# Two attention and mixture-of-experts layers on one core: the last four source tiles of the second attention go to target chunk 0 first, and two routed tiles are run among the products of the others

## What is computed

```
z = s1[:, None, :] + s2[None, :, :]              # 2048 x 2048 x 4 heads
e = where(z > 0, z, 0.2 * z).mean(-1)
attn = softmax(where(adj > 0, e, -9e15), axis=1)
x = x + attn @ Wh

h = relu(layernorm(x) @ Wi.T + bi)               # 256 wide, routed block
for l in range(2):                               # one expert per 32 rows
    h = relu(shared_l(h) + routed_l(h) + h)
x = x + h @ Wo.T + bo
```

## Time and profile before

| what | value |
|---|---|
| time, median of 3 runs | 642.82 us (642.39 to 643.41) |
| the profiled execution | 641.88 us, its span 640.1 us |
| busy, share of the span | PE 85%, PEld 67%, DVE 81%, ACT 58%, POOL 27% |
| chain that ended last, by engine | PE 52%, DVE 26%, ACT 14%, issue 5% |
| its largest line | DVE L1633, 15% |

### The profile page before, as it was taken

The page is one execution under the profiler, slowest core; times in us unless marked ns, Lnnn a source line. Parts: engine busy times, 40 slices in busy tenths (PEclk is TensorE's granted clock), DMA queues, the critical chain, the costliest instruction groups (busy, mean ns, idle before and its releaser), DMA issues.

```text
span 640.1 us, 13281 instructions
## 1 busy us (share of the span) xinstructions
PE 545.5 (85%) x5082; PEld 427.7 (67%) x5082; DVE 515.6 (81%) x907; ACT 372.2 (58%) x756; POOL 175.9 (27%) x186
## 2 busy tenths in 40 slices
PE   1876984999999999799998897999996756999985
PEld 1675972878775877766685575588786555566753
DVE  6799969997787857699949738899999898999420
ACT  1796893768885777685756836633421301565473
POOL 3301000075211100993522010121314000365741
PEclk9987995989998899998998999899999878899999
DMA  6484860022165156999599224020102844475750
GB/s 142 85 161 76 215 153 2 17 83 68 33 199 198 38 195 215 186 211 237 119 209 110 67 69 131 2 67 1 66 1 80 303 134 139 120 208 175 202 165 16
DMA packets 48857, 78.36 MB, mean 122 GB/s; under 512 B 5406, under 2 KB 24870, under 8 KB 48794
## 3 DMA queue, kind: packets, MB, share of 16 engines
q1 hardware_dynamic: 30714, 52.02, 26.0%
q0 software_dynamic: 15488, 22.02, 20.1%
q10 hardware_dynamic: 2592, 3.48, 2.0%
HBM read 80.61 MB, written 22.06 MB: 160 GB/s over the span
## 4 chain that ended last, share of the span: by engine, by line
PE 52%; DVE 26%; ACT 14%; issue 5%; DMA 1%; ACTq 1%; POOL 0%; SPq 0%; DVEq 0%
DVE arena L1633 15%; PE bank L698 11%; PE bank L710 11%; PE bank L627 10%; PE bank L863 5%; ACT arena L1137 5%; PE bank L824 2%; ACT maskT L1006 2%; PE bank L658 2%; PE bank L900 2%; ACT ysb L1089 1%; PE bank L808 1%; PE bank L576 1%; PE bank L603 1%; DVE arena L1489 1%
## 5 line engine op out<-in xcount | busy, mean ns | idle before, releaser
L483 POOL TENSOR_TENSOR x<-x,ysb 128x512 f32<-128x512 f32 x36 | 74.7, 2076 | 249.8 <-ACT ysb L1089 237.7
L1137 ACT ACTIVATE arena<-heads,nd 128x512 bf16<-128x512 f32 x176 | 112.0, 723 | 22.9 <-PE bank L627 22.3
L698 PE MATMUL bank<-hTc,arena 128*128 128x512 f32 x192 | 92.9, 638 | 5.6 <-ACT reg_c L1078 5.6
L1633 DVE SCALAR_TENSOR_TENSOR arena<-reg_b,nd,arena 128x1536 f32<-128x1536 f32 x48 | 92.0, 1979 | 0.0
L710 PEld LDWEIGHTS bank<-arena,reg_c 128*128 128x128 f32 x768 | 87.6, 192 | 4.8 <-issue 4.7
L710 PE MATMUL bank<-arena,reg_c 128*128 128x128 f32 x768 | 88.5, 275 | 0.0
L627 PEld LDWEIGHTS bank<-reg_b,arena 128*128 128x128 bf16 x1536 | 73.7, 99 | 7.1 <-DVE arena L1489 4.0
L1078 ACT ACTIVATE reg_c<-bank,b 128x512 f32<-128x512 f32 x96 | 65.0, 686 | 22.8 <-PE bank L698 22.6
L627 PE MATMUL bank<-reg_b,arena 128*128 128x99 bf16 x1536 | 74.9, 211 | 3.7 <-DVE arena L1489 3.7
L1089 ACT ACTIVATE ysb<-bank,comb 128x128 f32<-128x128 f32 x128 | 36.5, 367 | 65.0 <-PE bank L909 39.9
L1475 DVE TENSOR_TENSOR arena<-maskT,arena 128x2048 bf16<-128x2048 bf16 x36 | 50.4, 1401 | 27.4 <-ACT arena L1137 27.4
(11 more groups left out here) (195 smaller groups left out, 846.6 us busy)
## 6 DMA issues: line engine op xcount, KB each, us to landing
maskT<-routed_sums SPq DMA_DIRECT2D x48, 256.0 KB, 3.2
reg_c<-in_adj POOLq DMA_DIRECT2D x16, 512.0 KB, 7.9
arena<-in_w1T SPq DMA_DIRECT2D x16, 512.0 KB, 4.0
arena<-in_w2T SPq DMA_DIRECT2D x16, 512.0 KB, 4.9
routed_sums<-in_wsT SPq DMA_DIRECT2D x32, 256.0 KB, 5.6
routed_sums<-in_wrT POOLq DMA_DIRECT2D x32, 256.0 KB, 13.9
arena<-routed_sums SPq DMA_DIRECT2D x32, 256.0 KB, 3.0
routed_sums<-ident POOLq DMA_DIRECT2D x4, 1024.0 KB, 12.6
```

The lines of the kernel that those rows point to most:

```text
L483: nc.gpsimd.tensor_tensor(xi, xi, ysb[:, e % 3, :].rearrange("p (t d) -> p t d", d=P), ALU.add).then_inc(s_acc, 1)
L698: mm(bank[b][:, :], w1[:, s, e % 2, c * P:(c + 1) * P], hTc[:, :], start=True, stop=True).then_inc(full[b], 1)
L1137: last = af(ind[:, q, b, j, :], sbc[:, h, :], ACT.Relu, bias=nd[:, q * QT + j, h:h + 1], scale=BIG)
L1633: last = v.scalar_tensor_tensor(p, row, nd[:, t, h:h + 1], p if h else maskT[:, t, columns], ALU.max, ALU.mult)
```

## The change

The pass over source tiles 12 to 15 is split by targets. First come 512 columns (chunk 0) of all four tiles and all heads, then 1024 columns (chunks 1 and 2), head by head; chunk 0 is merged and normalised on DVE between the first and the second head of these. PE takes the four tiles to chunk 0's bank space, then chunk 0's first pair of routed tiles in banks of its own (4 to 7), then the four tiles to the other targets. The `attend1` tiles are spread otherwise over the pairs. The loads of `kept` 0 to 11 go ahead of the small weights; the second-layer weights of tiles 0 and 1 get places of their own. The diff, cut to its core:

```diff
         def w_second(t, g):
             m = t % 2 * GT + g
+            if t < 2:
+                return (arena[:, 8848:9360], arena[:, 9360:9872], hT[:, WW:N], ysb[:, 2, :],
+                        *(rows1[:, h, 0:CW] for h in range(H)))[m].rearrange("p (k n) -> p k n", k=KC)
...
+        def tile_banks(t):
+            return ((4, 5), (6, 7))[t] if t < 2 else (2 + t % 2 * 2, 3 + t % 2 * 2)
...
+            sp.wait_ge(s_skip, 16 * L * KC)
+            for e in range(T - CT):
+                load_kept(e)
             sp.wait_ge(s_acc, FFN_Y)
...
+            sp.wait_ge(ev["rows"], 3 * H)
+            load_second(0)
+            sp.wait_ge(s_c0, CT)
+            load_second(1)
+            for e in range(T - CT, E1):
+                load_kept(e)
             load_second(2)
             load_second(3)
             sp.wait_ge(full[3], BANK3)
-            load_second(0)
-            load_second(1)
...
+            def attend_part(targets, t, ready):
+                pe.wait_ge(s_v1, C)
+                pe.wait_ge(ready, t + 1 if ready is s_wide else t - (T - CT) + 1)
+                for i in targets:
+                    b, o = i // 3, i % 3 * (P + 1)
+                    last = mm(bank[b][:, o:o + P + 1], wide[:, t % 4, i * P:(i + 1) * P], v1[:, t, :], start=False,
+                              stop=(t == T - 1), skip_group_check=True)
...
-            for g in range(5, T // 2):
-                attend_wide(g)
-            attend1(0)
-            attend1(1)
+            attend_wide(5)
+            for t in range(T - CT, T):
+                attend_part(range(CT), t, s_c0)
...
-                    if l == 0 and then is not None:
+                    if l == at and then is not None:
                         ln_transpose(6, then)
...
             ln_transpose(6, odiv)
             expert_pair(0, 0, ((), (), ()))
-            expert_pair(0, 2, ((2,), (3,), ()), xn)
-            expert_pair(1, 0, ((), (4,), ()))
-            expert_pair(1, 2, ((5, 6, 7), (8,), ()), odiv)
-            expert_pair(2, 0, ((9, 10), (11, 12, 13), (14, 15)))
-            expert_pair(2, 2, ((), (), ()))
+            pe.wait_ge(s_c0sums, 1)
+            for t in range(T - CT, T):
+                attend_part(range(CT, WT), t, s_wide)
+            attend1(0)
+            attend1(1)
+            expert_pair(0, 2, ((), (), ()), xn, 1)
+            expert_pair(1, 0, ((2,), (3,), ()))
+            expert_pair(1, 2, ((4,), (5, 6), (7,)), odiv)
+            expert_pair(2, 0, ((8,), (9, 10), (11,)))
+            expert_pair(2, 2, ((12,), (13, 14), (15,)))
             ln_transpose(6, xn)
...
-            sums(*[3 * (P + 1)] * (WT // 3), to=reg_b)
+            act.wait_ge(s_attf, C * H)
+            got(0)
+            af(att[:, 0:3 * (P + 1)], bank[0][:, 0:3 * (P + 1)], ACT.Copy).then_inc(ev["att"], 1)
+            got(1)
+            af(att[:, 3 * (P + 1):CT * (P + 1)], bank[1][:, 0:P + 1], ACT.Copy).then_inc(s_c0sums, 1)
...
+                    if (c, i) == (C - 2, 2):
+                        sums(3 * (P + 1), P + 1)
+                    for t in pair:
+                        output(t)
+                    if (c, i) == (0, 0):
+                        act.wait_ge(s_kept, 16 * E1)
+                        select(3, range(GT))
+                        other_sums()
...
-            for g in range(6, T // 2):
-                wide_pair(g)
+            for g in (6, 7):
+                dve.wait_ge(s_exp, 3 + g // 2)
+                dve.wait_ge(s_widef, g - 1)
+                for h in range(H):
+                    products(h, (2 * g, 2 * g + 1), wide[:, :, 0:CW], rows1[:, h, 0:CW], slice(0, CW), s_c0)
+
+            def other_targets(h):
+
+                products(h, range(T - CT, T), wide[:, :, CW:WW], rows1[:, h, CW:WW], slice(CW, WW), s_wide)
+
+            other_targets(0)
+            dve.wait_ge(ev["att"], (2 * C + 1) * H + 1)
+            dve.wait_ge(s_c0sums, 1)
+            divisors(CT, att)
+            then(merge1(0, CT, 0, att))
+            norm(0, 2 * C + 4, odiv)
+            for h in range(1, H):
+                other_targets(h)
             dve.wait_ge(ev["rows"], 3 * H)
             dve.wait_ge(s_v1, C)
             last_tiles(0, 2)
 
             dve.wait_ge(ev["att"], (2 * C + 1) * H + WT // 3)
-            divisors(WT, reg_b)
-            then(merge1(0, CT, 0, reg_b))
-            norm(0, 2 * C + 4, odiv)
-            last_tiles(2, 2)
-            merge1(CT, 2 * CT, CT, reg_b).then_inc(s_attf, 1)
+            rest = reg_b[:, CW:]
+            divisors(2 * CT, rest)
+            merge1(CT, 2 * CT, 0, rest).then_inc(s_attf, 1)
...
             scale(CT, xn)
-            last_tiles(4, QT)
             dve.wait_ge(ev["hTc"], 2 * C + 5)
             scale(2 * CT, odiv, CT)
+            last_tiles(2, 2)
+            last_tiles(4, QT)
             last_tiles(8, QT)
             last_tiles(12, QT)
```

More of the change, by code:

```diff
@@ L408, in _ @@
             sp.wait_ge(full[3], BANK3)
-            load_second(0)
-            load_second(1)
-            for t in range(4, T):
-                sp.wait_ge(full[3 + t % 2 * 2], (BANK5 if t % 2 else BANK3) + (t - 4) // 2 * (L + 1) + L)
+            load_second(4)
+            load_second(5)
+            for t in range(6, T):
+                sp.wait_ge(*layer_done(t - 4, L - 1))
                 load_second(t)
@@ L808, in attend_wide @@
                         last = mm(bank[b][:, o:o + P + 1], wide[:, t % 4, i * P:(i + 1) * P], v1[:, t, :],
[L809 to L813, removed]
+                                  start=(t == 0 and i % 3 == 0), stop=False, skip_group_check=True)
+                last.then_inc(s_widef, 1)
+            def attend_part(targets, t, ready):
[5 more added lines that the diff above has]
+                              stop=(t == T - 1), skip_group_check=True)
+                    if t == T - 1 and (i % 3 == 2 or i == CT - 1):
+                        last.then_inc(full[b], 1)
             def attend1(t):
@@ L876, in turn, with output @@
                 last.then_inc(full[b], 1)
-            def output(i):
-                r, b = i % 2, 3 + i % 2 * 2
-                ready(b - 1)
+            def output(t):
+                r, (a0, b) = t % 2, tile_banks(t)
+                ready(a0)
                 use(b, "y")
@@ L958, in expert_pair @@
                 for t in pair:
-                    hidden(t % CT)
+                    hidden(t)
                 for l in range(L):
@@ L1287, in _, with other_sums, hidden @@
             scale_values(3)
-            sums(*[3 * (P + 1)] * (WT // 3), to=reg_b)
-            def hidden(i):
-                b = 2 + i % 2 * 2
+            act.wait_ge(s_attf, C * H)
[3 more added lines that the diff above has]
+            af(att[:, 3 * (P + 1):CT * (P + 1)], bank[1][:, 0:P + 1], ACT.Copy).then_inc(s_c0sums, 1)
+            k.event("sums")
+            def other_sums():
+                o = CW
+                for b in range(1, WT // 3):
+                    got(b)
+                    w = slice(P + 1 if b == 1 else 0, 3 * (P + 1))
+                    af(reg_b[:, o:o + w.stop - w.start], bank[b][:, w], ACT.Copy).then_inc(ev["att"], 1)
+                    o += w.stop - w.start
+            def hidden(t):
+                i, b = t % CT, tile_banks(t)[0]
                 got(b)
@@ L1297, in hidden, with layer, turn, output @@
                 last.then_inc(ev["htt"], 1)
[L1299 to L1300 removed]
+            def layer(t):
+                b = tile_banks(t)[1]
                 got(b)
[L1302 to L1305 removed]
+                af(hn[:, t % 2, :], bank[b][:, 0:HID], ACT.Relu).then_inc(ev["htt"], 1)
+            def turn(t, l):
+                b = tile_banks(t)[0]
                 got(b)
[L1307 to L1310 removed]
+                af(htt[:, t % 2, l + 1, :], bank[b][:, 0:HID], ACT.Copy).then_inc(ev["htt"], 1)
+            def output(t):
+                i, b = t % CT, tile_banks(t)[1]
                 y_slot(CT)
```

84 lines of the change are left out of this document (40 added, 44 removed).

## The result

The changed kernel takes 666.97 us (median of 4 runs, 665.3 to 669.71) against 642.61 for the kernel before on the same chip; the ratio is 1.0404, with a 95% interval of 1.0359 to 1.0448. It is slower, as forecast, but by 24 us instead of 5, and outside the range. The profiled execution took 666.59, span 664.8.

A forecast was written before the change was run, and what follows sets the result against it. DVE was taken to set the pace until 541.9, then PE and ACT alternately. First pair 16.1 us earlier, 10.3 given back, (2, 2) 5.0 ahead, then norm and clock: span +5.0, 647.8 us; range 643.0 to 651.2.

The forecast's parts named there:

- chunk 3's open norm: Between pairs (2, 2) and (3, 0): nothing covers merge and norm, costing 9.7 + 2.1 us against 1.8 before.
- DVE's front: DVE's split passes over tiles 12 to 15: 2.9 us slot wait, chunk 0 normalised at 525.7, first pair 16.1 us earlier.
- The others' products: Products for the other targets, behind the first pair: 10.3 of 16.1 us given back, pair (0, 2) starting at 548.9.
- The step that failed: POOL beside DVE's passes: DVE loses 0.41 us per us of POOL, 2.3 us and later 6.6.
- The fourth rival: POOL excludes DVE for whole instructions in the other targets' passes: 3.3 us more, 651.1 us in all; chance 0.12.
- The moved scaling: DVE's scaling of chunk 2, ahead of the 14 remaining tiles: costs its duration, 1.3 us.
- The term of the turn-taking: DVE's 56 passes for 14 tiles: 37.5 us plus 6.6 for some 16 us of POOL, through at about 602.
- the forecast's 144.3: Forecast length from the first pass over tile 12 to the span's end: 645.1 - 500.8.
- the five middle pairs: Pairs (0, 2) to (2, 2): 56.5 to 58.4 us plus waits, ending at 608.2, 5.0 ahead of before.
- four slots 2 in use: Middle pairs: `attend1` tiles in four slots where PE waits for ACT anyway, not one; may save up to 2 us.

The follow-up runs named there:

- run 14: Changed kernel, DVE waiting for each head's passes to end, tiles 12 to 15 in slot 0 of pair (2, 2), ACT copies earlier: 648.43 us, ratio 1.011.
- Run 4: Kernel before, only chunk 2's scaling moved from behind tiles 4 to 7 to ahead of tile 4: 653.19 us against 642.44.
- run 9: Changed kernel, DVE waiting for each head's passes to end before the next head, in chunk 3's and the 1024-column passes: 652.26 us, ratio 1.0158.
- run 1: Changed kernel, second operand of chunk 3's passes behind tile 1 read from PSUM, so its attention is not computed: 643.48 us beside 642.44.
- run 13: Changed kernel, chunk 3's second operand from PSUM, tiles 12 to 15 in slot 0 of pair (2, 2), ACT copies earlier: 642.73 us, ratio 1.0028.
- runs 3 and 7: Changed kernel: one with POOL's tile 6 and 8 copies before additions, 664.77 us; other with waits between heads, tiles 12 to 15 earlier, 651.77 us.

## Why the prediction was wrong

Its direction came true, and the term that it gave for the sign, chunk 3's open norm, has the forecast size. But that term does not decide the sign: with the norm covered and no hold left the whole change is still slower (run 14: part 144.2 against 139.3, ratio 1.011). And the size lacks a mechanism, POOL held, that is worth more than all of its terms.

- **DVE's front: right.** The wait was 2.65 us (forecast 2.9), released by `attend_wide(5)`. Passes of 1024 columns took 1.195 (taken: 1.20). `odiv` was ready and the first pair started at 525.1 (forecast 525.7), behind 8.14 us of idle.
- **The others' products: right in the sum, by two errors that cancel.** `hidden` of pair (0, 2) started at 548.66, forecast 548.9. The forecast had 5.6 us of POOL beside the twelve 1024-column passes and 2.3 us lost. The window of the changed kernel, 524.93 to 541.94, has 10.43 us of POOL, since its four copies took 6.24 there, and 2.7 us lost (17.01 instead of 12 x 1.195): 0.26 per us, not 0.41.
- **The step that failed** is the one that priced POOL beside DVE: "At 0.41: +2.3", and again "plus POOL at 0.41 per us for some 16 us of it, 6.6". It asks only what POOL costs DVE. The engine that lost was POOL, and it was on the path through `select(6)`. The fourth rival had the engines exclude each other for whole instructions, but put the loss on DVE too, at 651.1. The Trainium skill (SBUF — State Buffer, Who interferes with whom) says that whoever issues first has the shared ports for its whole instruction and the other is blocked fully. This trace agrees that POOL was blocked, but for 24.5 us, over 37 of DVE's instructions; the wait for one of them would be 0.7.
- **The moved scaling was costed at its duration**: "Then DVE scales chunk 2 (1.3) and makes 14 tiles". What it was to POOL where it stood before was not asked. Run 4 puts that at 14.7 us by itself, in one profile.
- **The sign of it was in the trace of before**, and I did not draw on it. POOL's timeline of the kernel before:

```profile
567.05 2.31 POOL L550 TENSOR_TENSOR x<-x,ysb 128x128 f32<-128x128 f32 x2 [4.92 <-ACT ysb L1313]
...
590.37 6.50 POOL L550 TENSOR_TENSOR x<-x,ysb 128x128 f32<-128x128 f32 x2 [6.70 <-ACT ysb L1313]
```

and DVE's, of the same stretch:

```profile
568.55 1.40 DVE L1383 TENSOR_SCALAR odiv<-x,means,rstd 128x128 f32<-128x128 f32 x4
...
593.41 2.73 DVE L1633 SCALAR_TENSOR_TENSOR arena<-ysb,nd,arena 128x512 f32<-128x512 f32 x4
```

  Two additions that take 0.87 alone took 2.31 and got through as the scaling ran; two others took 6.50, and the first of them was still running at 595.9, just before DVE's last pass ended at 596.1. Nobody waited for either, so they cost nothing and looked like nothing. The forecast priced POOL from two windows, and both rows lie outside these.
- **The term of the turn-taking was mis-sized as well.** With POOL let in (run 9) DVE is through 105.9 us behind its first pass over tile 12; the forecast has 602 - 500.8 = 101.2. The price per us was about right (0.37 to 0.42 measured, for 0.41); the amount of POOL beside it was 26.2 us, not 16: undisturbed it would be some 18, by run 1's durations, and taking turns lengthens it.
- **Chunk 3's norm: right.** Idle of 7.71 us (forecast 7.9), clock 0.50 behind it, and pair (3, 0) 11.4 long (forecast 11.1). Covering it gave 5.8 (run 13 over run 1) and 4.2 (run 14 over run 9).
- **A hit that isn't one.** Run 1's 144.0 is close to the forecast's 144.3, but in tiles 2 to 15 run 1 has neither holds nor turn-taking, and the forecast had 6.6 us of the latter on DVE. With both engines sharing and no hold the part is 148.4, and run 9's `hidden` of (3, 0) is at 121.7, the forecast's at 117.1. Of these 4.6 us, 2.2 are there at the start of (0, 2), at 50.3 for 48.1; the five middle pairs take 61.9 for the forecast's 59.3. The forecast also counts four slots 2 in use, where the change's lists have three, with tiles 7, 11 and 15.

**What stays open.** What decides whether a POOL instruction gets its first turn: the same bias addition took 1.4 to 2.0 us in most runs and 16.48 and 20.45 in two, and a copy at 558.37 in the trace of before got in at once where run 4's at 554.26 didn't. How the arrival falls between two passes doesn't settle it, as far as the traces resolve it. POOL's bias addition in runs 3 and 7:

```profile
528.31 2.00 POOL L567 TENSOR_TENSOR x<-x,arena 128x512 f32<-128x512 f32 x1 [33.36 <-DMA maskT<-routed_sums]
```

```profile
529.77 16.48 POOL L567 TENSOR_TENSOR x<-x,arena 128x512 f32<-128x512 f32 x1 [33.39 <-DVE odiv L1436]
```

Each starts 0.23 us behind the first of the twelve 1024-column passes (528.08 and 529.54); one got in behind that pass, the other was held. In all runs where it got in, it ended some 2.2 us behind the start of that pass, wherever it had arrived (0.23 to 0.82 us behind it). Open too is why the stretch ahead of tile 12 differs by up to 7 us between profiles.

## What to carry to other kernels

Before a short DVE operation is moved out of a long row of two-input SBUF passes, ask which POOL instruction gets its turn in that place, and who waits for it; where POOL is on the path, leave a gap in every group of passes (a wait for a completion cost 0.05 to 0.12 us here; the turn-taking that it lets in costs more), or read one operand from PSUM, which was tried here only with an operand that leaves a result out. In a trace, look for POOL instructions far longer than their kind whose end falls on the moment at which DVE stops or changes its operation: they are harmless only until somebody waits for them. Starting an expensive block earlier is worth what is left when its displaced work has been paid for: here 16 us of earlier start came to 1 in one profile (run 13, without sharing), and to no gain in any time.

## What the runs showed of the hardware

- POOL instructions that read SBUF, with one input or two, were held for up to 24.5 us while DVE ran passes with two SBUF inputs back to back at 0.665 us each; DVE lost nothing in that time. Not every one is held: what decides it is open.
- A wait for the completion of the last pass, or one DVE operation with one SBUF input, was enough to let it in. Once in, consecutive POOL instructions took turns with DVE's passes: four copies 4.0 us instead of 2.62, DVE losing about 0.4 us per us of POOL. Beside 1024-column passes the four copies took 6.24, and DVE lost 0.26 per us.
- With the second operand in PSUM, a 128x512 pass takes the same 0.66 us, and POOL's instructions their undisturbed times.
- An idle of 2.04 us of PE was already followed by 0.50 of the clock at once (run 13), while behind 2.03 us the clock was still 1.00 and fell within the next 2 us (run 14); the forecast had reasoned from idles of 4 to 7.
